# Deformable and ternary convolution chain on one core: matmuls of the 3x3 convolutions leave out the padding row at an image's edge

## The reference, cut to what matters

```python
# block 0: deformable convolution
om = conv3x3(gn(x), w_off) + b_off              # 27 offset and mask channels, padding 1
sampled = bilinear samples of gn(x) at the shifted points, times sigmoid(mask)
y = group_norm16(einsum(sampled, weight) + bias) * gamma + beta
x = x + y
# block 1: two convolutions with weights quantised to -1, 0, 1
xn = gn(x)
out1 = relu(batchnorm(conv3x3(xn, q1)))         # padding 1
out2 = batchnorm(conv3x3(out1, q2))             # padding 1
x = x + relu(out1 + out2)
```

## Time and profile before

| What | Value |
|---|---|
| median of 3 runs | 316.64 us |
| lowest, highest | 316.12, 319.75 us |
| the profiled execution's own time | 319.02 us |
| its span, first to last instruction | 317.3 us |
| mean granted TensorE clock in the span | 0.966 |

### The profile page before, as it was taken

The page is one execution under the profiler, slowest core; times in us unless marked ns, Lnnn a source line. Parts: engine busy times, 40 slices in busy tenths (PEclk is TensorE's granted clock), DMA queues, the critical chain, the costliest instruction groups (busy, mean ns, idle before and its releaser), DMA issues.

```text
span 317.3 us, 4982 instructions
## 1 busy us (share of the span) xinstructions
PE 275.5 (87%) x1708; PEld 241.4 (76%) x1708; DVE 209.7 (66%) x416; ACT 176.5 (56%) x333; POOL 144.7 (46%) x195
## 2 busy tenths in 40 slices
PE   2889999799999999989989989988799948999800
PEld 2768787699989899989989989986677736777600
DVE  3778666779988999578878788771363434115195
ACT  2429653788867978877798677850043015330051
POOL 7440376476666777977558964240000004211063
PEclk9999999999999999999999999999799995999975
DMA  7800966934332332333322333000000000000015
GB/s 244 322 0 3 299 215 176 276 119 140 101 116 88 119 91 82 104 106 107 108 67 93 113 112 106 20 1 7 2 0 0 2 0 1 0 2 0 0 64 201
DMA packets 24887, 28.60 MB, mean 90 GB/s; under 512 B 2445, under 2 KB 22525, under 8 KB 24856
## 3 DMA queue, kind: packets, MB, share of 16 engines
q1 hardware_dynamic: 24640, 27.50, 26.9%
q10 hardware_dynamic: 216, 0.71, 0.7%
HBM read 19.87 MB, written 6.78 MB: 84 GB/s over the span
## 4 chain that ended last, share of the span: by engine, by line
PE 70%; DVE 16%; ACT 9%; issue 2%; DMA 1%; DVEq 0%; ACTq 0%
PE PS L669 24%; PE PS L528 10%; PE PS L557 9%; PE PS L593 4%; PE PS L595 4%; PE PS L594 4%; PE PS L575 4%; PE PS L577 4%; PE PS L576 4%; DVE slo L1129 3%; DVE st L1033 2%; DVE vlo L1136 2%; ACT vhi L818 2%; ACT shi L811 2%; DVE xb L1416 2%
## 5 line engine op out<-in xcount | busy, mean ns | idle before, releaser
L447 POOL TENSOR_TENSOR vt<-rowm,hat 128x1026 f32<-128x1026 f32 x36 | 70.8, 1967 | 37.5 <-PE PS L557 36.8
L1129 DVE TENSOR_TENSOR slo<-PS,shi 114x512 fp32r<-114x512 f32 x72 | 53.5, 751 | 12.4 <-ACT shi L811 12.2
L1136 DVE TENSOR_TENSOR vlo<-PS,vhi 128x576 fp32r<-128x576 f32 (+2 forms) x84 | 50.2, 618 | 12.2 <-ACT vhi L818 12.1
L811 ACT ACTIVATE shi<-PS 114x512 fp32r<-114x512 f32 x72 | 46.3, 652 | 20.3 <-PE PS L557 20.0
L557 PE MATMUL PS<-ident,vt 128*114 128x128 f32 x324 | 47.4, 275 | 1.6 <-DVE nsm L996 0.7
L818 ACT ACTIVATE vhi<-PS 128x576 fp32r<-128x576 f32 (+2 forms) x84 | 44.1, 546 | 7.2 <-PE PS L577 4.9
L669 PE MATMUL PS<-xhi,q 128*128 128x512 f32 x144 | 41.0, 434 | 5.1 <-ACT xhi L967 5.1
L575 PE MATMUL PS<-shi,patch 114*128 114x288 f32 x136 | 43.7, 322 | 1.9 <-DVE omh L1227 1.5
L593 PE MATMUL PS<-vhi,wdhi 128*128 128x256 f32 x144 | 43.0, 299 | 2.1 <-ACT xb L825 2.0
L576 PE MATMUL PS<-slo,patch 114*128 114x288 f32 x136 | 40.7, 299 | 0.0
L577 PE MATMUL PS<-shi,patch 114*128 114x288 f32 x136 | 40.6, 298 | 0.0
(11 more groups left out here) (141 smaller groups left out, 474.0 us busy)
## 6 DMA issues: line engine op xcount, KB each, us to landing
patch<-xt SPq DMA_DIRECT2D x136, 114.0 KB
xt<-xtt SPq DMA_DIRECT2D x4, 1024.0 KB, 6.7
xs<-in_x SPq DMA_DIRECT2D x4, 512.0 KB, 7.2
out<-xb SPq DMA_DIRECT2D x8, 256.0 KB, 2.0
wraw<-in_L_conv_w SPq DMA_DIRECT2D x2, 576.0 KB, 10.0
omr<-omr SPq DMA_DIRECT2D x8, 128.0 KB, 4.6
wd_raw<-in_L_conv_weight ACTq DMA_DIRECT2D x1, 576.0 KB, 8.0
omr<-omr SPq DMA_DIRECT2D x4, 124.0 KB, 4.2
```

The source lines that it names most:

```text
L447: g.tensor_tensor(vt[:, n % 2, :, :].rearrange("p t (r j) -> p t r j", r=WR), rowm[:, n % 2, :, :].unsqueeze(3).to_broadcast([P, TAPS, WR, ...
L811: a.activation(shi[:, n % 2, lo:hi], S_PS[:, lo:hi], ACT.Copy).then_inc(shi_ok, 1)
L1129: d.tensor_tensor(slo[:, n % 2, lo:hi], S_PS[:, lo:hi], shi[:, n % 2, lo:hi], ALU.subtract).then_inc(slo_ok, 1)
L1136: last = d.tensor_tensor(places(vlo), src, places(vhi), ALU.subtract)
```

## The change

Each tap's matmul gets an explicit range of rows, on the output and on the input. For h = 0 the taps of the first kernel row cover image rows 1 to 15 of the chunk and leave out row 0; for h = 1 the taps of the last kernel row cover the first 15 rows and leave out the last. The row left out would have been multiplied with the zero frame. All other taps cover 16 rows. The columns stay 32 wide in every tap. So 3 of 9 matmuls in every part have 480 columns, not 512.

[...] The small matmuls inside the offset convolution stay at the same place in the count. No instruction, wait or semaphore is added or taken away.

```diff
+        TAP_ORDER = [[K + 1] + [k for k in range(TAPS) if k != K + 1], [k for k in range(TAPS) if k != K + 1] + [K + 1]]
+
+        def tap_rows(h, k):
+            return (1 if (h, k // K) == (0, 0) else 0), H // 2 - (1 if (h, k // K) == (1, K - 1) else 0)
+
+        def tap_cols(k):
+            return 0, W
+
+        def tap_out(m, h, k):
+            (r0, r1), (c0, c1) = tap_rows(h, k), tap_cols(k)
+            return square(m)[:, r0:r1, c0:c1]
+
+        def tap_in(img, b, h, k):
+            (r0, r1), (c0, c1) = tap_rows(h, k), tap_cols(k)
+            r, c = b % RING * ROWS + h * (H // 2) + k // K, k % K
+            return img[:, r + r0:r + r1, c + c0:c + c1]
...
-                    for k in range(TAPS):
-                        r = b % RING * ROWS + h * (H // 2) + k // K
-                        last = t.matmul(OFF_PS[(2 * b + h) % 4], woffT[:, k, :], src[:, r:r + H // 2, k % K:k % K + W],
-                                        start=(k == 0 and part == 0), stop=(k == TAPS - 1 and part == 1))
-                        if (b, h, part, k) == (0, 0, 1, 4):
+                    for i, k in enumerate(TAP_ORDER[part]):
+                        last = t.matmul(tap_out(OFF_PS[(2 * b + h) % 4], h, k), woffT[:, k, :], tap_in(src, b, h, k),
+                                        start=(i == 0 and part == 0), stop=(i == TAPS - 1 and part == 1))
+                        if (b, h, part, i) == (0, 0, 1, 4):
                             group_mean(GN0, 1)
-                        if (b, h, part, k) == (0, 1, 0, 2):
+                        if (b, h, part, i) == (0, 1, 0, 2):
                             group_square(GN0, 1)
...
-                for k in range(TAPS):
-                    r = b % RING * ROWS + h * (H // 2) + k // K
-                    last = t.matmul(PS[:, 2 * b + h, :], q[:, k, :], src[:, r:r + H // 2, k % K:k % K + W],
-                                    start=(k == 0 and part == 0), stop=(k == TAPS - 1 and part == 1))
+                for i, k in enumerate(TAP_ORDER[part]):
+                    last = t.matmul(tap_out(PS[:, 2 * b + h, :], h, k), q[:, k, :], tap_in(src, b, h, k),
+                                    start=(i == 0 and part == 0), stop=(i == TAPS - 1 and part == 1))
```

## The result

| | before | changed |
|---|---|---|
| median, lowest to highest (22 runs each) | 318.84, 316.12 to 319.86 us | 316.30, 314.57 to 318.37 us |
| profiled execution: its time, its span | 319.02, 317.3 us | 315.29, 313.6 us |
| mean granted clock in that span | 0.966 | 0.966 |

The ratio of the changed kernel to the one before is 0.9941, with an interval of 0.9919 to 0.9963: faster by 0.6%, some 1.9 us (the two medians lie 2.5 us apart), within the 2% that I called "same". The median of 316.3 us lies in my range of 313.4 to 317.3, but 1.8 us above the 314.5 that I forecast, and the kernel before did not stand where its first three runs had put it: its median is 318.84, not 316.64.

The account below looks back on a forecast made before the run. TensorE's 512-column convolution matmuls were taken as the bound. 130 x 15.25 ns = 1.98 us plus 0.22 us made 2.20 us; off the median 316.64 this gave 314.44, rounded to 314.5 us, range 313.4 to 317.3.

Parts of the forecast that it names:

- What bounds the kernel, and that all of it arrives: Where the convolutions' 512-column matmuls stand, they are the bound; savings there arrive: 0.64, 0.77 and 0.79 us by stage.
- Price of one: In the convolutions, one row of 32 columns left out saves 15.25 ns, with ends of 13.3 and 17.4 ns.
- What the 31 ns on top are: Convolution matmuls stand 244 ns apart; the 31 ns above the columns' 213.3 were put to 16 row runs, 1.9 ns each.
- the rival of the broken output: Convolution outputs count as 16 or 15 runs at 1.9 ns each, costing 13.0 us: 327 us; chance 0.02.
- The order, the view, the weights: In the convolutions, tap order, output view and kept weight loads cost nothing; the order's bound is below 0.1 us.
- What is late next: The image turn's 0.50 us wait shrinks by 0.09; patches hardly move; all 0.64 us of the offset convolution pass through.
- Price at the lower clock: In two low-clock stretches of the ternary convolutions, 8 short matmuls at 27.8 ns a row save 0.22 us.
- Against which time: For the whole kernel, 2.20 us off the profiled 319.02 gives 316.82; off the median 316.64 gives 314.44 us.
- The rival of a longer low clock: After the gaps before the ternary convolutions, more matmuls at the low clock, 200 ns each: 317.3 us; chance 0.19.
- What a measurement can tell: For the whole kernel, a difference of 2% (6.3 us) is about what a measurement can tell from none.

Follow-up runs that it names:

- the order alone: Changed kernel with all taps at 16 rows again, keeping its tap order and output view: 317.18 us against 318.26 for the kernel before, ratio 0.9978.
- the ternary side alone: Short matmuls only in the two ternary convolutions, offset convolution as in the kernel before: 317.49 us against 318.26, ratio 0.9961.
- The filled kernels: Kernel before and changed kernel, each with 20 matmuls added in the first batch norm's gap: first 315.57 and 313.62 us against 318.19 for the kernel before.
- pieces of 30 words: Changed kernel with left and right taps covering 30 of 32 columns, so output is in separate runs: 313.41 us against 318.26 for the kernel before.
- the fastest group: Runs with the highest mean granted clock, nothing edited: kernel before at 0.970 to 0.971, median 316.92 us; changed kernel at 0.966 to 0.967, median 315.37 us.
- the second pair: Kernel before and changed kernel, each with the same 20 gap matmuls, on another chip: 316.68 and 314.60 us against 318.07 for the kernel before.

## Why the prediction was right or wrong

*What bounds the kernel, and that all of it arrives*: right. The three convolution stages became shorter by 0.61, 0.70 and, free of clock, 0.65 to 0.70 us, against 0.64, 0.77 and 0.79 foreseen, and the deformable part kept its length within 0.1 us. The first chunk of the offset convolution saved nothing in these profiles. It isn't always off the path, though: in the profiles of the order alone and of the ternary side alone the chain runs through its last 14 matmuls up to the small one, which comes at 16.22 and 16.76 there. In such an execution its 6 short matmuls, some 0.08 us, would count too.

*Price of one*: mis-sized a little at most. I took 15.25 ns for a row. The filled kernels give (35.44 - 34.74) / 48 = 14.6 ns and (35.42 - 34.77) / 48 = 13.5 ns in the second convolution, the stretch of 72 gives (17.68 - 17.39) / 24 = 12 ns, all of the first ternary convolution at the full clock 0.60 / 45 = 13.3 ns, the offset stage 0.61 / 42 = 14.5 ns. All lie in or near the range of 13.3 to 17.4, and nearer to the columns alone. At 14 ns, 138 are 1.93 us. With more rows left out the chunks give (4.40 - 4.03) / 24 = 15.4 and (4.40 - 3.67) / 48 = 15.2 ns a row, which is my price. One row is too little to tell 13.3 from 15.25 with these stages, and it moves the sum by 0.3 us.

*What the 31 ns on top are*: wrong in part. I put all of them down to the 16 row runs, 1.9 ns each. The matmuls of the filled gap read 512 words in one piece and still start 230 ns apart, so 17 of the 31 ns are there without any rows, and a run costs a little under 1 ns (last section). The forecast did not hang on it; the rival of the broken output did, and it was half as dear by this price.

*The order, the view, the weights*: right. The order alone changed nothing, pieces of 30 words cost 2 to 4 ns, and chunks with 256-column matmuls came out at 3.67 us, so a weight load sets no floor at 229 ns.

*What is late next*: the image turn at 23.98 and the patches held in the changed kernel, and with four rows left out the turn did cost 0.2 us, as its cover of 0.50 us said it would. I did not name the wait with the longest story behind it: the pixel store of 7.14 us and the `xtt` copies. It did no harm at 0.6 us, nor at 2.5 us, and made TensorE wait at 5 us.

*Price at the lower clock*: the size was near, 4.00 - 3.93 = 0.07 us for the three short ones among the nine that open the second ternary convolution (260.01 to 263.94 in the timeline of after), 23 ns each for my 27.8. But I booked it as part of the change. The short matmuls of 0.22 us in such stretches depend on where a stretch falls; in the profiled execution of after there was none in chunk (0, 1).

*Against which time*: this is the step that failed. The sum against the profiled execution gave 316.82 us, and the median came to 316.3. I then read the 2.38 us between that execution and the median of three as low-clock matmuls that a usual run doesn't have, and took 2.2 us off 316.64. The runs show the contrary. Of 22 runs before, the median is 318.84, near the profiled 319.02. In the table, 44 of 69 runs of the kernel before stand below the fastest group, and the profiled execution's 0.966 is the clock of the largest one, so low clock of that order is in the usual run. By their times 316.12 and 316.64 belong to the fastest group; their clocks are not on record. From 318.84 the same 2.2 us lead to 316.64, and 316.30 was measured; from 316.64 they led to 314.44. I had even the evidence in hand, as two of four executions stood at 319 or above, and counted three of them.

*The rival of a longer low clock* was not what happened, though its time, 317.3, was nearer than mine: nothing shows that the change lengthened the stretches. They were in both kernels, the fastest group holds about as large a share of the runs in either (25 of 69, 14 of 34), and with the gap filled the second convolution alone is 2.3 us shorter in the kernel before (35.44 against 37.72) and 2.1 us in the changed one (34.74 against 36.82). TensorE: Matmul & The Clock Gate of the Trainium skill, Part 1, says that the point of change varies from run to run; the groups in the table agree.

*What a measurement can tell*: I wrote about 2%. With 22 runs on each side the interval was 0.2% to either side of the ratio, and it told 0.6% from none.

## What to carry to other kernels

Where one engine is busy without a gap and the chain runs over it, a saving of 0.6% can be foreseen within some tenths of a us by counting instructions on the path and pricing one by the distance between starts; check it by stages of the trace, because the times of runs spread by more. Before a sum is set against a median, ask how many runs the median has and whether the profiled one is a usual run: here the two medians of before lie 2.2 us apart, as much as the whole change was foreseen to be worth. And look at the clock after each gap of the busiest engine: filling one gap with idle work gave as much as the change itself, and both together the fastest of the kernels here that leave nothing of the computation out.

## What the runs showed of the hardware that I had not expected

Twenty matmuls whose result nobody reads kept the granted clock at 1.00 through a gap of 5.1 us; without them the next nine matmuls took 4.00 us, with them 2.30. The stall at the branch, 1.8 to 2.4 us long, was followed by a stretch at the lower clock in some executions and not in others (nine matmuls in 3.47 us in the profile of before, 2.25 us in that of the changed kernel). Of the 13 profiles of this study 9 have it, behind stalls of 1.76 to 2.39 us, and 4 don't, behind stalls of 1.90 to 2.10 us, so the length of the stall does not decide it. How often it comes is what differs between the two chips on which the filling gave 2.6 and 1.4 us; why it comes more often on one stays open.

The distance between two matmuls of 512 columns depends on how the moving operand lies. The twenty filling matmuls read 512 words in one piece, each with a 128x128 weight load and at a granted clock of 1.00. The first starts at 255.58, and with this one three are left:

```profile
259.49 0.84 PE L748 MATMUL PS<-wdlo,wdhi 128*128 128x512 f32 x3
```

That is 3.91 us for 17 distances, 230 ns each, and the second pair has the same 3.91 us. The convolutions' matmuls read 16 rows of 32 words and stand 244 ns apart. So 14 ns go with the 16 pieces, a little under 1 ns each; that it is the pieces and nothing else in the operand is the nearest reading, not shown by an edit of its own. It fits that eight rows less saved 122 ns, 15.2 ns a row, more than the 13.3 ns of the columns, while 32 columns taken off as two from each of 16 rows saved only 0.13 us / 12 = 11 ns: there no piece of the input went away, and the output came in pieces. These two causes were not separated.
